# Second layer's key steps behind the links of its queries' chain, and two value chunks between its last first maxima

## The chip, the cores and the metric

The kernel runs on one core of one Trainium2 chip. The metric is the device time of one execution in microseconds; lower is better. The engines are TensorE (PE in the rows, its weight loads PEld), VectorE (DVE), ScalarE (ACT), GpSimd (POOL) and SyncE (SP), which issues the transfers.

## The reference

Two layers of a small perceiver work on 64 tokens x of 128 features and a context of 6272 rows. Each layer adds three blocks to x: cross-attention to the context, self-attention, and a mixture of experts.

```python
x = x + xattn0(layernorm(x), ctx)      # 16 heads of 8; q = y Wq + bq, k = ctx Wk + bk, v = ctx Wv + bv
x = x + attn0(layernorm(x))            # causal, 16 heads of 64
x = x + ffn0(layernorm(x))             # 8 experts, top 2, and a gated shared one
x = x + xattn1(layernorm(x), ctx)      # as xattn0, with q and k of each head normalised:
                                       #   qh = layernorm(qh, q_gamma, q_beta) * scale; kh = layernorm(kh, k_gamma, k_beta)
x = x + attn1(layernorm(x))            # rotary
x = x + ffn1(layernorm(x))             # 32 experts, top 1, and a shared one
```

The change lies where `ffn0` ends and `xattn1` begins.

## The kernel before

The context stands transposed in SBUF, 49 tiles of 128 rows, worked in NB = 13 chunks of up to 512 columns (the last has one tile). Each engine has its own instruction stream, written out by hand; the order in a stream is the order of the work, and semaphores tie the streams together.

**Keys of the second layer.** They don't depend on x, so they are made in steps that are placed among the serial links of `attn0` and `ffn0`. There are STEPS = 28. Step 2c is key chunk c: TensorE multiplies it (two records of 512 columns), ScalarE writes it twice, scaled into `klo` and squared into `khi`. Step 2c+1 is variance chunk c-1: TensorE averages the squares within each head, ScalarE turns them by Ln and Exp into 1/std (`k_rstd`). Then GpSimd multiplies (`k_scaled`, line 389), and VectorE adds beta, rounds and splits the result into a high and a low part (lines 581 and 584, `k_split`), after which SyncE copies both into the stacked form `kst`. On TensorE and ScalarE, `keys_until(n)` does the steps up to n that aren't done yet; the tables `PE_KEYS` and `ACT_KEYS` say up to which step at which named place. `DVE_KEYS` does so by chunks for VectorE. `PE_KEYS_IN_MAXIMA` and `DVE_KEYS_IN_MAXIMA` do it behind or ahead of the numbered pairs of the first maxima.

**Queries of the second layer.** After `ffn0`, x is normalised and transposed (`yT_of("ln3")`, copied by VectorE at line 539). TensorE multiplies by the centred query weights (`q1_ps`), ScalarE squares (line 493, `q1_sq`), TensorE averages (`q1_var`), ScalarE does Ln and Exp (lines 496, 497, `q1_std`), VectorE scales, adds beta and splits (lines 744 to 747, `q1_n`), TensorE spreads the result over rows (`query_rows`), and VectorE and ScalarE copy half each into `qst` (lines 544 and 449, `q_ready`).

**First maxima.** For head group 0, 13 pairs of score matmuls (`max_pair`) give each query's maximum over a chunk; VectorE reduces each pair (line 548). Between the pairs TensorE makes key steps and value chunks (`VALUES_IN_MAXIMA`), which ScalarE copies into `vaug` (`v_out`, line 402). `VALUE_BANKS` gives each value chunk's PSUM bank. Then come the shift (the maximum is subtracted from the queries) and the steps of the main loop (`cross`): scores, exponential (line 436), weighted sum, while the maxima of the next group run in slots of their own (line 554). The last LAST_V = 2 value chunks stand in the loop's first step, behind the first scores; scores 0 wait until all but these are copied, scores 1 until all are.

**Fill.** `keep_busy(n, free)` issues n matmuls of 256 columns into the free bank `free`; their result isn't used.

SyncE's order in the second layer: stack copies of groups 0 and 1, then the expert weights for the end of the kernel, then the stack copies of groups 2 and 3.

Of the kernel before, what the change touches and what calls it, by code (L numbers as in the profile page):

```python
# [16 lines left out]
NG = 4  # L17
# [104 lines left out]
def score_user(B):  # L122
# [5 lines left out]


STEPS = 2 * (NB + 1)  # L130
PE_KEYS = {"drain": 1, "o": 3, "x1": 6, "yT1": 7, "scores": 10, "probs": 11, "z": 12, "proj": 15, "ln2": 17, "y": 19,
           "yT3": 20, "q1": 21, "n1": 23}
PE_KEYS_IN_MAXIMA = {1: 24, 2: 25, 3: 26, 5: STEPS}
ACT_KEYS = {"drain": 3, "scores": 7, "vs": 12, "tab": 13, "sig": 17, "ln3": 19, "var": 20}
DVE_KEYS = {"ln1": 1, "qk": 2, "turned": 3, "z": 4, "h": 5, "hT": 6, "q1": 7, "n1": 8}
DVE_KEYS_IN_MAXIMA = {0: 9, 2: 10, 4: 11, 5: 12, 6: NB}

VALUE_BANKS = (5, 6, 3, 3, 1, 0, 1, 0, 1, 0, 1, 3, 2)
VALUES_IN_MAXIMA = {1: (2,), 3: (3,), 5: (4, 5), 6: (6,), 7: (7,), 8: (8,), 9: (9,), 12: (10,)}

ONE_VAR_BANK = 10
def var_bank(c):
# [6 lines left out]
def v_schedule(c):  # L149


    done = [0, 0, 1, 1, 2, 2] + [2 + min(6, -(-2 * n // 3)) + max(0, 3 * (n - 8) // 4) for n in range(NB)] + [NB - LAST_V]
    at = c + KEYS_AHEAD
    return range(done[at - 1] if at else 0, done[at] if c + 1 < NB else NB - LAST_V)

LAST_V = 2


def v_bank(l, c):
# [25 lines left out]
def perceiver(nc, ctxT, packs, experts, out):  # L187
    with ExitStack() as ctx:
# [202 lines left out]
        def _(act):  # L391
# [7 lines left out]
            def v_out(l, c):  # L399
                k = tiles(c)  # L400
                act.wait_ge(v_proj, l * NB + c + 1)
                nc.scalar.activation(vaug[:, BT * c:BT * c + k, :, 0:DH],  # L402
                                     ps[:, v_bank(l, c), 0:k * D].rearrange("p (t h d) -> p t h d", t=k, h=H),
                                     ACT.Copy).then_inc(v_set, 1)
# [22 lines left out]
            def exps(l):  # L427
                for g in range(NG):
                    for i in range(NB):
                        G = NG * l + g  # L430
                        B = G * NB + i
                        if B >= PROBS:
                            act.wait_ge(av_done, B - PROBS + 1)
                        act.wait_ge(scores_done, B + 1)
                        b0, w = score_bank(B), tiles(i) * P
                        nc.scalar.activation(prob[:, B % PROBS, :].rearrange("p (u c) -> p u c", u=2)[:, :, 0:w],  # L436
                                             ps[:, b0:b0 + 2, 0:w], ACT.Exp, scale=XSCALE).then_inc(exp_done, 1)
                        if g >= 1 and i == 0:
                            act.wait_ge(av_done, NB * G)
                            if G >= 2:  # L440
                                act.wait_ge(o_ready, G - 1)
                            nc.scalar.activation(avsb[:, :], ps[:, ACC, 0:GQ], ACT.Copy).then_inc(acc_copied, 1)
                        if g == 0 and i == 0:
                            for v in range(NB - LAST_V, NB):
                                v_out(l, v)
            def stack_queries(l):
                act.wait_ge(ev(f"q{l}_rows"), 1)
# [39 lines left out]
            nc.scalar.preload_act_table_set("natural_log_exp_and_others")  # L487
            keys_until(ACT_KEYS["sig"])
            v_out(1, 0)
            norm_std("ln3")  # L490
            keys_until(ACT_KEYS["ln3"])
            act.wait_ge(ev("q1_ps"), 1)
            nc.scalar.activation(q_n[:, 0:T], ps[:, 4, GQ:GQ + T], ACT.Square, bias=bq1c[:, 0:1]).then_inc(ev("q1_sq"), 1)
            keys_until(ACT_KEYS["var"])
            act.wait_ge(ev("q1_var"), 1)
            link(nc.scalar.activation(q_n[:, T:2 * T], ps[:, 4, GQ + T:GQ + 2 * T], ACT.Ln, bias=eps_col[:, 0:1]))
            nc.scalar.activation(q_n[:, T:2 * T], q_n[:, T:2 * T], ACT.Exp, scale=-0.5).then_inc(ev("q1_std"), 1)
            v_out(1, 1)
            stack_queries(1)
            keys_until(24)  # L500
            v_out(1, 2)
            keys_until(26)
            v_out(1, 3)
            keys_until(STEPS)
            for c in range(4, NB - LAST_V):
                v_out(1, c)
            exps(1)
            norm_std("ln4")
# [335 lines left out]
        def _(pe):  # L844
# [81 lines left out]
            def scores(G, i):  # L926
                B = NB * G + i
                if i == 0:
                    pe.wait_ge(shift_ready, 2 * (G + 1))
                if G % NG == 0 and i == 1:  # L930

                    pe.wait_ge(v_set, (G // NG + 1) * NB)
                if G % NG == 0 and i == 0:
                    pe.wait_ge(v_set, G // NG * NB + NB - LAST_V)
                elif G % NG == NG - 1 and i == 2:

                    pe.wait_ge(max_read, (G // NG + 1) * READS_OF_LAYER)
                elif score_user(B) is not None:
                    pe.wait_ge(exp_done, score_user(B) + 1)
                for t in range(tiles(i)):  # L940
                    a = (BT * i + t) * P
                    for p in range(2):
                        r = slice(p * HALF, (p + 1) * HALF)
                        last = one(ps[:, score_bank(B) + p, t * P:(t + 1) * P], kst[r, G % 2, a:a + P],
                                   qst[r, G % NG, p * P:(p + 1) * P])
                last.then_inc(scores_done, 1)
# [24 lines left out]
            def cross(l, wv):  # L971
                G0 = NG * l
                for s in range(EARLY_SLOTS):
                    max_slot(l, s)
                before = []
                for n, (front, back) in enumerate(STEP_SLOTS):
                    g, j = divmod(n, len(STEPS_OF_GROUP))
                    here = [(G0 + g, i) for i in STEPS_OF_GROUP[j]]
                    for s in front:
                        max_slot(l, s)  # L980
                    for G, i in here:
                        scores(G, i)
                    if n == 0:
                        for v in range(NB - LAST_V, NB):
                            v_chunk(l, v, wv)
                    for m, s in enumerate(back):
                        max_slot(l, s)
                        if n == 0:

                            if m == 0:  # L990
                                pe.wait_ge(v_set, (l + 1) * NB - 1)
                            keep_busy(2, 3)
                    for G, i in before:
                        weighted(G, i)
                    if j == 1 and g >= 1:
                        gather(G0 + g - 1)
                    if l == 1 and g == NG - 1 and j == 1:
                        pe.wait_ge(max_read, 2 * READS_OF_LAYER)
                        nc.tensor.transpose(ps[:, 7, 0:T], view["bv1"], ident[0:T, 0:T]).then_inc(ev("bias1_T"), 1)
                    if l == 1 and g == NG - 1 and j == 2:  # L1000
                        pe.wait_ge(ev("bias1_Ts"), 1)
                        one(ps[0:T, 7, D:2 * D], attT[:, :], view["wp1"]).then_inc(ev("bias1_out"), 1)
                    if l == 0 and g == NG - 1 and j == 1:

                        pe.wait_ge(in_pack["raw1"], 16)
                        pe.wait_ge(max_read, READS_OF_LAYER)
                        one(ps[:, 7, 0:D], view["wk1"], view["cen"])
                        one(ps[:, 7, D:D + 1], view["cen"], view["bk1"])
                        for q in range(NG):
                            one(ps[q * GC:(q + 1) * GC, 7, D + 1:D + 2], view["cen"][0:QROWS, 0:GC], view["bq1x3"][:, q:q + 1])  # L1010
                        one(ps[QROWS:P, 7, D + 2:D + 4], ident[0:QROWS, 0:GC], view["qgb"])
                        one(ps[:, 7, D + 4:2 * D + 4], view["wq1"], view["cen"]).then_inc(ev("l1_ps"), 1)
                    before = here
                if l == 0:

                    pe.wait_ge(ev("l1_weights"), 1)
                    keys_until(PE_KEYS["drain"])
                for G, i in before:
                    weighted(G, i)
                if l == 0:  # L1020
                    keep_busy(1, 7)
                gather(G0 + NG - 1)
# [99 lines left out]
            last.then_inc(ev("ffn0_hT"), 1)  # L1122
            pe.wait_ge(in_pack["small1"], 16)
            v_chunk(1, 0, view["wv1"])
            keep_busy(1, 4)
            pe.wait_ge(ev("ffn0_hTs"), 1)
            for e in range(E0 + 1):
                hh, k = e // SL, e % SL
# [3 lines left out]
            keys_until(PE_KEYS["y"])  # L1132
            v_chunk(1, 1, view["wv1"])
            yT_of("ln3")
            keys_until(PE_KEYS["yT3"])
            one(ps[:, 4, GQ:GQ + T], wq1c[:, :], yT[:, :]).then_inc(ev("q1_ps"), 1)
            keys_until(PE_KEYS["q1"])
            pe.wait_ge(ev("q1_sq"), 1)
            one(ps[:, 4, GQ + T:GQ + 2 * T], view["avg"], q_n[:, 0:T]).then_inc(ev("q1_var"), 1)
            keys_until(PE_KEYS["n1"])  # L1140

            pe.wait_ge(v_set, NB + 2)

            pe.wait_ge(k_rstd, 9)
            keep_busy(2, 2)
            query_rows(1)
            keep_busy(2, 2)
            pe.wait_ge(q_ready, 4)
            for c in range(NB):
                max_pair(1, c)  # L1150
# [187 lines left out]
```

## Time and profile before

| | |
|---|---|
| runs | 308.15 us median of 3 (306.65 to 308.65) |
| profiled execution | 308.23 us |
| span of its trace | 306.4 us |
| mean granted clock of TensorE | 0.989 |
| busy: TensorE, VectorE, ScalarE, GpSimd | 285.7, 211.8, 170.9, 29.5 us |

The span runs from the first to the last instruction in the trace, and starts and ends inside the time. A busy time is that of one engine; the engines overlap, so the shares say little on what sets the end. Almost every TensorE instruction is recorded at line 847, the helper `one`, so it is told apart by its tiles: `arena,consts` is a variance chunk, `arena,wk1c` a key chunk, `small,arena` a value chunk, `kst,qst` with 512 columns a maxima pair, `consts` alone a fill.

### The profile page before, as it was taken

To read this page: it belongs to the slowest core of one execution; us is meant where nothing else is said; L and a number is where in the kernel's file an instruction comes from. 1 tells how busy PE (TensorE), PEld (TensorE's weight loads), DVE (VectorE), ACT (ScalarE), POOL (GpSimd) and SP (SyncE) were. 2 spreads that over 40 slices of the span, in tenths; PEclk is the share of its full clock that TensorE was granted. 3 is DMA by queue.
4 is the path that set the end of the run, shared out by engine and by line. 5 is a ranking of instruction groups with operands and counts; after the bars stand their busy time and mean duration, and the time that the engine had idled before them with its cause. 6 is when DMAs were issued, how large, how long until landed. Compare 5 with 4: busy or idle time off the path is not lost.

```text
span 306.4 us, 8390 instructions
## 1 busy us (share of the span) xinstructions
PE 285.7 (93%) x3619; PEld 204.1 (67%) x3619; DVE 211.8 (69%) x443; ACT 170.9 (56%) x236; POOL 29.5 (10%) x23
## 2 busy tenths in 40 slices
PE   8999999999999998998899879999999998989986
PEld 4545667778787873554547656777877786556765
DVE  3679979899895104767879975989989411457762
ACT  3654337767666786579778322776767695031000
POOL 7710000000000002151325000000000000000000
PEclk9999999999999999999999977999999999999999
DMA  7877996756600370203065699994679600000000
GB/s 240 318 152 150 189 206 135 149 114 120 125 2 2 105 340 0 49 22 89 0 128 90 138 291 424 338 249 116 119 157 497 297 3 4 0 0 2 1 2 4
DMA packets 8116, 41.12 MB, mean 134 GB/s; under 512 B 2192, under 2 KB 2512, under 8 KB 7568
## 3 DMA queue, kind: packets, MB, share of 16 engines
q1 hardware_dynamic: 7936, 40.32, 47.9%
q8 instruction: 28, 0.46, 0.6%
q10 hardware_dynamic: 144, 0.27, 0.3%
q14 instruction: 8, 0.07, 0.1%
HBM read 21.29 MB, written 0.03 MB: 70 GB/s over the span
## 4 chain that ended last, share of the span: by engine, by line
PE 71%; DVE 18%; ACT 4%; DMA 3%; issue 2%; SPq 1%; DVEq 0%; ACTq 0%
PE ps L847 70%; DVE mx L548 4%; DVE mx L554 2%; DVE arena L584 2%; DMA arena<-in_ctxT 2%; ACT prob L436 1%; DVE arena L581 1%; DMA kst<-arena 1%; DVE arena L590 1%; DVE vaug L837 0%; ACT arena L408 0%; ACT arena L425 0%; ACT arena L424 0%; DVE qst L560 0%; SPq L319 0%
## 5 line engine op out<-in xcount | busy, mean ns | idle before, releaser
L436 ACT ACTIVATE prob<-ps 128x1024 f32<-128x1024 f32 (+1 forms) x104 | 99.5, 975 | 43.3 <-PE ps L847 43.1
L554 DVE TENSOR_REDUCE mx<-ps 128x1 f32<-128x512 f32 (+1 forms) x156 | 95.1, 655 | 14.5 <-PE ps L847 10.1
L847 PEld LDWEIGHTS ps<-qst,kst 64*128 64x128 f32 x784 | 53.1, 188 | 6.7 <-issue 1.8
L847 PE MATMUL ps<-prob,vaug 128*18 128x128 f32 x1568 | 57.0, 274 | 0.1
L847 PE MATMUL ps<-kst,qst 64*128 64x512 f32 (+1 forms) x208 | 50.5, 483 | 6.3 <-DVE mx L554 2.4
L847 PE MATMUL ps<-qst,kst 64*128 64x128 f32 x784 | 54.5, 273 | 0.7 <-ACT prob L436 0.3
L847 PEld LDWEIGHTS ps<-prob,vaug 128*18 128x18 f32 x1568 | 41.0, 97 | 9.9 <-issue 6.8
L847 PEld LDWEIGHTS ps<-kst,qst 64*128 64x128 f32 x208 | 19.9, 184 | 25.7 <-issue 13.2
L548 DVE TENSOR_REDUCE mx<-ps 128x2 f32<-128x1024 f32 (+1 forms) x26 | 29.2, 1156 | 0.7 <-PE ps L847 0.4
L402 ACT ACTIVATE vaug<-ps 128x512 f32<-128x512 f32 (+1 forms) x26 | 14.6, 571 | 19.6 <-PE ps L847 19.5
L847 PE MATMUL ps<-consts 128*128 128x256 f32 (+2 forms) x78 | 23.1, 416 | 0.0
L389 POOL TENSOR_TENSOR arena<-arena 128x512 f32<-128x512 f32 (+1 forms) x13 | 16.4, 1264 | 36.4 <-ACT arena L425 36.4
L847 PEld LDWEIGHTS ps<-consts 128*128 128x128 f32 (+1 forms) x78 | 13.5, 194 | 5.0 <-issue 2.1
L847 PE MATMUL ps<-arena,vaug 128*64 128x256 f32 (+1 forms) x184 | 15.6, 327 | 1.0 <-DVE vaug L837 0.8
L847 PEld LDWEIGHTS ps<-arena,vaug 128*64 128x64 f32 x184 | 12.8, 137 | 3.8 <-DVE vaug L837 1.3
L847 PEld LDWEIGHTS ps<-small,arena 128*128 128x128 f32 x98 | 13.0, 205 | 3.1 <-issue 1.4
L847 PE MATMUL ps<-small,arena 128*128 128x128 f32 x98 | 14.6, 298 | 0.1
L847 PE MATMUL ps<-arena,w 128*128 128x512 f32 (+1 forms) x26 | 13.9, 632 | 0.4 <-DVE arena L590 0.3
L847 PE MATMUL ps<-arena,consts 128*128 128x512 f32 (+1 forms) x26 | 13.6, 605 | 0.7 <-DVE yT L539 0.3
L575 DVE COPY avsb<-ps 128x256 f32<-128x256 f32 x2 | 0.8, 424 | 19.4 <-PE ps L847 19.4
L847 PEld LDWEIGHTS ps<-w,arena 128*128 128x128 f32 x98 | 12.0, 191 | 3.1 <-issue 2.9
L847 PE MATMUL ps<-w,arena 128*128 128x128 f32 x98 | 13.9, 285 | 0.0
(214 smaller groups left out, 267.7 us busy)
## 6 DMA issues: line engine op xcount, KB each, us to landing
kst<-arena SPq DMA_DIRECT2D x48, 192.0 KB, 3.6
kst<-arena SPq DMA_DIRECT2D x48, 128.0 KB, 2.7
arena<-in_experts SPq DMA_DIRECT2D x1, 5760.0 KB, 18.5
kst<-arena SPq DMA_DIRECT2D x24, 144.0 KB, 3.2
w<-in_experts SPq DMA_DIRECT2D x1, 3456.0 KB, 11.8
w<-in_late SPq DMA_DIRECT2D x1, 3284.5 KB, 11.4
arena<-in_experts SPq DMA_DIRECT2D x1, 3072.0 KB, 14.2
arena<-in_ctxT SPq DMA_DIRECT2D x2, 768.0 KB, 8.1
```

Source lines behind the costliest of these rows:

```text
L389: nc.gpsimd.tensor_tensor(klo[:, a:b], klo[:, a:b], khi[:, a:b], ALU.mult).then_inc(k_scaled, 1)
L402: nc.scalar.activation(vaug[:, BT * c:BT * c + k, :, 0:DH], ps[:, v_bank(l, c), 0:k * D].rearrange("p (t h d) -> p t h d", t=k, h=H), ACT. ...
L436: nc.scalar.activation(prob[:, B % PROBS, :].rearrange("p (u c) -> p u c", u=2)[:, :, 0:w], ps[:, b0:b0 + 2, 0:w], ACT.Exp, scale=XSCALE). ...
L548: V.tensor_reduce(mx[:, :, k], ps[:, pair_bank(k):pair_bank(k) + 2, 0:width(k)], AX, ALU.max).then_inc(max_read, 1)
L554: V.reduce_max(mx[:, p, k:k + 1], ps[:, bank(s, p), 0:width(k)], AX).then_inc(max_read, 1)
L575: V.tensor_copy(avsb[:, :], ps[:, ACC, 0:GQ]).then_inc(acc_copied, 1)
L581: V.tensor_scalar(khi[:, a:b].bitcast(F32R), klo[:, a:b], view["kgb"][:, 1:2], None, ALU.add).then_inc(k_full, 1)
L584: V.scalar_tensor_tensor(klo[:, a:b], klo[:, a:b], view["kgb"][:, 1:2], khi[:, a:b], ALU.add, ALU.subtract).then_inc(k_split, 1)
L590: V.scalar_tensor_tensor(klo[:, a:b], ps[:, c % 2, 0:width(c)], view["bk0"], khi[:, a:b], ALU.add, ALU.subtract).then_inc(k_split, 1)
L847: return mm(out_, lhsT, rhs, start=start, stop=stop, skip_group_check=True)
```

## The change

Four edits, all in the second layer.

- Steps on TensorE: variance chunk 7 (step 17) takes the place of the fill behind value chunk 0; key chunk 9 and variance chunk 8 (steps 18, 19) stand behind the last matmuls of `ffn0`; no step stands between the transposed input and the query matmul, or between this and the average; steps 20 and 21 come behind the average, step 22 behind the query rows. The wait for `k_rstd` 9 and the four fills around the query rows go.
- Steps on ScalarE: step 17 comes ahead of the norm's Ln, step 18 stays behind it, and step 19 goes from ahead of the queries' Ln to behind value chunk 1's copy.
- Value chunk 10 goes from behind pair 12 to behind pair 11, and chunk 11 from the first step of the loop to behind pair 12. `LAST_V` becomes (2, 1), one number for each layer.
- In the first step of the second layer's loop, the fill is 3 matmuls behind each of two slots instead of 2.

```diff
-PE_KEYS = {"drain": 1, "o": 3, "x1": 6, "yT1": 7, "scores": 10, "probs": 11, "z": 12, "proj": 15, "ln2": 17, "y": 19,
-           "yT3": 20, "q1": 21, "n1": 23}
+PE_KEYS = {"drain": 1, "o": 3, "x1": 6, "yT1": 7, "scores": 10, "probs": 11, "z": 12, "proj": 15, "ln2": 17, "hT": 18,
+           "y": 20, "n1": 22, "rows": 23}
 PE_KEYS_IN_MAXIMA = {1: 24, 2: 25, 3: 26, 5: STEPS}
-ACT_KEYS = {"drain": 3, "scores": 7, "vs": 12, "tab": 13, "sig": 17, "ln3": 19, "var": 20}
+ACT_KEYS = {"drain": 3, "scores": 7, "vs": 12, "tab": 13, "sig": 17, "v0": 18, "ln3": 19, "v1": 20}
-VALUES_IN_MAXIMA = {1: (2,), 3: (3,), 5: (4, 5), 6: (6,), 7: (7,), 8: (8,), 9: (9,), 12: (10,)}
+VALUES_IN_MAXIMA = {1: (2,), 3: (3,), 5: (4, 5), 6: (6,), 7: (7,), 8: (8,), 9: (9,), 11: (10,), 12: (11,)}
...
-LAST_V = 2
+LAST_V = (2, 1)
...
             keys_until(ACT_KEYS["sig"])
             v_out(1, 0)
+            keys_until(ACT_KEYS["v0"])
             norm_std("ln3")
             keys_until(ACT_KEYS["ln3"])
             act.wait_ge(ev("q1_ps"), 1)
             nc.scalar.activation(q_n[:, 0:T], ps[:, 4, GQ:GQ + T], ACT.Square, bias=bq1c[:, 0:1]).then_inc(ev("q1_sq"), 1)
-            keys_until(ACT_KEYS["var"])
             act.wait_ge(ev("q1_var"), 1)
...
             v_out(1, 1)
+            keys_until(ACT_KEYS["v1"])
             stack_queries(1)
...
-                    pe.wait_ge(v_set, G // NG * NB + NB - LAST_V)
+                    pe.wait_ge(v_set, G // NG * NB + NB - LAST_V[G // NG])
...
-                        for v in range(NB - LAST_V, NB):
+                        for v in range(NB - LAST_V[l], NB):
                             v_chunk(l, v, wv)
...
-                            keep_busy(2, 3)
+                            keep_busy(2 + l, 3)
...
             v_chunk(1, 0, view["wv1"])
-            keep_busy(1, 4)
+            keys_until(PE_KEYS["hT"])
             pe.wait_ge(ev("ffn0_hTs"), 1)
...
             yT_of("ln3")
-            keys_until(PE_KEYS["yT3"])
             one(ps[:, 4, GQ:GQ + T], wq1c[:, :], yT[:, :]).then_inc(ev("q1_ps"), 1)
-            keys_until(PE_KEYS["q1"])
             pe.wait_ge(ev("q1_sq"), 1)
             one(ps[:, 4, GQ + T:GQ + 2 * T], view["avg"], q_n[:, 0:T]).then_inc(ev("q1_var"), 1)
             keys_until(PE_KEYS["n1"])
 
             pe.wait_ge(v_set, NB + 2)
-
-            pe.wait_ge(k_rstd, 9)
-            keep_busy(2, 2)
             query_rows(1)
-            keep_busy(2, 2)
+            keys_until(PE_KEYS["rows"])
             pe.wait_ge(q_ready, 4)
```

The other uses of `LAST_V` follow in the same way.

## Rows read from the trace of the kernel before

**Rows 1.** The page: clock in 40 slices, then the chain by engine and line.

```profile
PEclk9999999999999999999999977999999999999999
...
PE 71%; DVE 18%; ACT 4%; DMA 3%; issue 2%; SPq 1%; DVEq 0%; ACTq 0%
PE ps L847 70%; DVE mx L548 4%; DVE mx L554 2%; DVE arena L584 2%; DMA arena<-in_ctxT 2%; ACT prob L436 1%; DVE arena L581 1%; DMA kst<-arena 1%; DVE arena L590 1%; DVE vaug L837 0%; ACT arena L408 0%; ACT arena L425 0%; ACT arena L424 0%; DVE qst L560 0%; SPq L319 0%
```

**Rows 2.** Timeline, 146 to 159 us: start, us, engine, line, instruction.

```profile
146.11 0.60 PE L847 MATMUL ps<-consts 128*128 128x256 f32 x2
...
147.45 1.31 PE L847 MATMUL ps<-w,prob 128*64 128x128 f32 x18 [0.74 <-DVE prob L736]
...
150.43 0.29 ACT L453 ACTIVATE lnv<-mv,eps_col 64x1 f32<-64x1 f32 x1 [1.77 <-DVE mv L534]
...
151.80 0.22 DVE L539 COPY yT<-ps 128x64 f32<-128x64 f32 x1 [0.40 <-PE ps L863]
...
152.08 1.12 PE L847 MATMUL ps<-arena,consts 128*128 128x512 f32 x2 [0.32 <-DVE yT L539]
...
153.41 0.31 ACT L493 ACTIVATE prob<-ps,bq1c 128x64 f32<-128x64 f32 x1
...
154.87 0.30 ACT L496 ACTIVATE prob<-ps,eps_col 128x64 f32<-128x64 f32 x1
...
155.81 0.55 DVE L745 TENSOR_SCALAR qhl<-prob,qgb 128x64 fp32r<-128x64 f32 x1
...
156.28 0.30 DVE L746 TENSOR_SCALAR prob<-prob,qgb 128x64 f32<-128x64 f32 x1
...
156.62 0.23 DVE L747 TENSOR_TENSOR qhl<-prob,qhl 128x64 fp32r<-128x64 f32 x1
...
157.06 0.53 PE L847 MATMUL ps<-qhl,spread 32*128 32x64 f32 x12
...
157.94 0.84 DVE L544 CAST qst<-ps 32x256 fp32r<-32x256 f32 x2
```

**Rows 3.** Busy us by stage, columns PE, PEld, DVE, ACT, POOL, clock, DMA, GB/s.

```profile
158.80:180.00 21.20, 17.83 (x106) 12.21 (x106) 20.64 (x26) 12.26 (x23) 4.41 (x4) 1.00 0.69 132
```

**Rows 4.** Busy us of six stretches, columns as in rows 3.

```profile
181.30:189.01 7.71, 7.71 (x30) 5.47 (x30) 3.53 (x6) 1.79 (x3) 0.00 (x0) 0.59 0.93 394
39.40:44.40 5.00, 4.96 (x30) 3.44 (x30) 3.53 (x6) 1.79 (x3) 0.00 (x0) 1.00 1.00 234
189.01:242.60 53.59, 51.84 (x947) 41.19 (x947) 47.06 (x88) 37.12 (x40) 0.00 (x0) 1.00 0.85 272
44.40:97.96 53.56, 51.81 (x947) 41.19 (x947) 47.05 (x88) 37.11 (x40) 0.00 (x0) 1.00 0.46 96
177.00:181.30 4.30, 2.54 (x19) 1.49 (x18) 3.59 (x8) 0.60 (x1) 0.00 (x0) 0.93 1.15 274
...
292.50:296.70 4.20, 3.08 (x24) 1.69 (x20) 3.28 (x10) 0.47 (x1) 0.00 (x0) 1.00 0.00 0
```

**Rows 5.** One microsecond on TensorE: busy us, granted clock, DMA share, GB/s.

```profile
181.00:182.00 1.00, 0.88 (x9) 0.50 1.27 429
```

**Rows 6.** The chain of waits: a two-record matmul with nothing ahead.

```profile
273.46 0.45 PE ps L847 x2
```

**Rows 7.** Timeline, 132 to 135 us: VectorE and GpSimd meet.

```profile
132.85 0.75 DVE L584 SCALAR_TENSOR_TENSOR arena<-arena,consts 128x512 f32<-128x512 f32 x1
...
133.15 1.60 POOL L389 TENSOR_TENSOR arena<-arena 128x512 f32<-128x512 f32 x1 [1.21 <-ACT arena L425]
```

**Rows 8.** Timeline, the end of the first maxima.

```profile
176.83 2.69 DVE L548 TENSOR_REDUCE mx<-ps 128x2 f32<-128x1024 f32 x3 [0.24 <-PE ps L847]
178.11 0.33 PE L847 MATMUL ps<-kst,qst 64*128 64x128 f32 x2 [0.97 <-DVE mx L548]
178.37 1.16 PE L847 MATMUL ps<-small,arena 128*128 128x128 f32 x8
...
180.19 0.41 PE L847 MATMUL ps<-consts,mhl 128*32 128x128 f32 x4 [0.66 <-DVE mhl L569]
```

More of the change, by code:

```diff
@@ L149, in v_schedule @@
 def v_schedule(c):
-    done = [0, 0, 1, 1, 2, 2] + [2 + min(6, -(-2 * n // 3)) + max(0, 3 * (n - 8) // 4) for n in range(NB)] + [NB - LAST_V]
+    done = [0, 0, 1, 1, 2, 2] + [2 + min(6, -(-2 * n // 3)) + max(0, 3 * (n - 8) // 4) for n in range(NB)] + [NB - LAST_V[0]]
     at = c + KEYS_AHEAD
-    return range(done[at - 1] if at else 0, done[at] if c + 1 < NB else NB - LAST_V)
-LAST_V = 2
+    return range(done[at - 1] if at else 0, done[at] if c + 1 < NB else NB - LAST_V[0])
+LAST_V = (2, 1)
 def v_bank(l, c):
@@ L504, in _ @@
             keys_until(STEPS)
-            for c in range(4, NB - LAST_V):
+            for c in range(4, NB - LAST_V[1]):
                 v_out(1, c)
@@ L983, in cross @@
                     if n == 0:
-                        for v in range(NB - LAST_V, NB):
+                        for v in range(NB - LAST_V[l], NB):
                             v_chunk(l, v, wv)
```

## The prediction

> **What bounds the kernel now.** I read the page's chain first: the tensor engine holds 71% of the chain that ended last and VectorE 18% [rows 1]. So a gain must come from a stretch where VectorE or a serial chain sets the pace, or where TensorE is slow. The clock row of the same page shows one such place: the granted clock is below full in two slices, about 176 to 191 us, and nowhere else inside the work [rows 1]. Then I read the timeline between the first layer's last stage and the second layer's first scores, because the whole change lies there. It has three parts.
>
> The **queries' chain** (149 to 159 us) is serial: normalised x is turned, multiplied by the query weights, squared, averaged, put through Ln and Exp, scaled, spread over rows and copied into qst. Key steps stand in front of its links. The turned input is ready at 152.02 (151.80 + 0.22), but TensorE first runs a variance chunk (152.08, 1.12 us), so the square of the queries starts only at 153.41; another key chunk stands before the average matmul, and the Ln starts at 154.87 [rows 2]. In the **first maxima** (158.8 to 180) VectorE is busy 20.64 of 21.20 us [rows 3]: it sets the pace, and whatever moves its first instruction moves the end. Then the **first scores**: from 181.30 to 189.01 TensorE takes 7.71 us for 30 matmul records. The first layer does the same work, same count, in 5.00 us (39.40 to 44.40) at full clock; here the mean granted clock is 0.59 [rows 4]. From 181 to 182 us the level is 0.50 (1.2 instead of 2.4 GHz) [rows 5], so the fall comes just before the first scores. Before it TensorE was busy for only 2.54 of 4.30 us (177.00 to 181.30) [rows 4]: it waits for the last first maxima and then for the shift.
>
> Behind 189.01 the layers are alike: 53.59 us against 53.56 to the end of their maxima [rows 4]. So what is won ahead of 189.01 should stay won.
>
> **The profiled execution** took 308.23 us for a span of 306.4, so 1.8 lie around the span; it is within 0.1 us of the median, 308.15. I sum against 308.23. A difference below about 1% (3.1 us) is what a measurement of this kernel hardly tells from none.
>
> **Part 1: the fill matmul behind the first value chunk becomes a variance chunk.** The fill costs some 0.53 us, the chunk some 1.1. It stands in a wait: value chunk 0 is through at about 146.2, the fill behind it (its first records at 146.11) ends at 146.71, and the matmuls that wait for hTs start at 147.45 [rows 2], so 1.1 us just fit. Price 0, up to 0.1 if the fit fails. Its Ln and Exp on ScalarE now come before the norm's Ln: ScalarE idles 1.77 us before that Ln [rows 2], they take 1.3. GpSimd's product for that key chunk then falls at about 150.0 to 151.3, beside VectorE's norm. The y instruction starts at 151.06 and would be held by at most the 0.25 us that L745 lost beside GpSimd (0.55 against 0.30 for the same shape) [rows 2]; I take 0, since the other work is short and reads ahead of GpSimd's end. The Trainium skill (GPSIMD Engine Reference, section 1, Specifications) says that GpSimd shares its SBUF interface with VectorE and contends with two-port modes and with instructions with two SBUF inputs. By that rule y may wait and the sum would be up to 0.25 worse.
>
> **Part 2: the queries' links no longer wait for key steps.** A two-record matmul with nothing in front took 0.45 us [rows 6]. So the square starts at 152.02 + 0.05 + 0.45 = 152.5 (before 153.41), and the Ln at 152.8 + 0.05 + 0.45 = 153.3 (before 154.87): 1.55 us. ScalarE must be free: its key chunk 9 starts right behind the norm at 150.9 and takes 1.35, done by 152.2. L745 ran beside GpSimd; GpSimd's next product is now later, so 0.25 comes on top: L747 ends at 156.85 - 1.55 - 0.25 = 155.05 [rows 2]. On TensorE key chunk 10 and variance chunk 9 now stand between the average matmul and the query rows: 153.25 + 2 x 0.93 = 155.1, just ready. With them go the wait for k_rstd and four fills. The query rows start 1.95 earlier than 157.06 [rows 2]. On VectorE key chunk 7 stands before its qst copies as before, so the copies end 1.8 earlier than 158.78 (157.94 + 0.84) [rows 2].
>
> What is late next: the product for key chunk 8. Its Ln and Exp now follow the queries' and value chunk 1 on ScalarE: 153.9 + 0.55 + 1.3 = 155.7. GpSimd starts then, beside VectorE's L584 of chunk 7 (155.5 to 156.25). In the like place GpSimd ended at 134.75 (133.15 + 1.60), 1.15 us behind an L584 that ended at 133.60 [rows 7]: so 157.4. VectorE, free at 157.0, starts chunk 8 at 157.45, against 158.81 (0.03 behind its copies). **Gain 1.4 us.** Key steps 20 to 23 on ScalarE follow the stack copies as before and come about 1.9 us earlier, so they don't hold VectorE later. One collision is left: the products of chunks 9 to 12 come earlier relative to VectorE by 0.5 us, and a meeting of the two stretches one of them, as here GpSimd's to 1.60 [rows 7]; there are such meetings now as well, so I take 0 and keep a loss of up to 0.9 for the range. Bounds of this part: 0 (all of it eaten by the two engines meeting) and 1.95 (the whole advance of the query rows).
>
> **Part 3: value chunk 10 a place earlier, chunk 11 behind the last first maxima.** Chunk 10 (8 records, 1.16 us) [rows 8] now goes between pairs 11 and 12. Pair 12 starts at 178.11 and would then start at about 178.2, while VectorE's last three reductions run from 176.83 to 179.52 without a gap, the last of them, pair 12's, a short one of some 0.35 [rows 8]: hidden, with 0.6 to spare. Chunk 11 runs from 178.55 to 179.7; the shift's matmul waits for VectorE until 180.19 anyway [rows 8]. The scores at 181.30 now wait for chunk 11's copy as well: 179.7 + 0.6 = 180.3, done. Without that cover each costs up to 1.1 us. In the first scores 8 records of a chunk go and two fills come (3 instead of 2, twice): 1.06 us out, 1.06 in, at full clock. Cost 0. The second scores wait for the copy of chunk 12, ready before, as it is now one short copy behind the first exponential.
>
> **Part 4: the clock.** With the two chunks TensorE's waits between 177.1 and 181.3 shrink from 1.76 us (4.30 - 2.54) to about 0.9: busy share 0.59 before, about 0.8 after. The trace shows full clock through 4.20 us with 3.08 busy (0.73, from 292.50) [rows 4]. So I take it that the clock stays up, and the first scores take the first layer's 5.00 us: **gain 2.7 us**. Bounds: 0 (still falls) and 2.7. Inside the new queries' chain the fills are gone, and two waits of 0.4 us and one of 0.3 lie within 151.7 to 153.3; key chunks fill both sides, so the busy share there stays above 0.7.
>
> The rule that speaks against the change is in TensorE: Matmul & The Clock Gate, Part 1: the Trainium skill says that the gated clock is the default, that only activity releases it, and that the monitor runs free of the kernel's start. By it the taking away of fills can cost the clock elsewhere, and the same program can fall in one execution and not in the next. The sum would then be 306.8 instead of 304.1.
>
> **Transfers.** SyncE's stack copies of the second layer wait for k_split, which comes with VectorE's key chunks: 1.4 earlier, like the pairs that read them. The expert loads follow them in SyncE's order, one of them behind the last value copy, and the stacks of groups 2 and 3 follow those. TensorE's need for these moves 4.1 us earlier and their issue follows the scores that free their slots, but the loads ahead of them move by only 1.4 to 4. If they landed just in time now, up to 2.7 us would be at risk; but the second layer, with the expert loads in the queue, is only 0.03 us longer behind 189.01 than the first, which has none there [rows 4], and DMA holds 3% of the chain, of which the stacks 1% [rows 1]. I take 0.
>
> **Sum.** 308.23 - 1.4 - 2.7 = 304.1 us.
>
> **Rivals.**
> - *The clock gain alone, 305.5.* The queries' chain moves but VectorE doesn't, as GpSimd's products or ScalarE's Ln and Exp come late. For: my margins at chunk 8 and at the query rows are under 0.5 us. Against: VectorE has at most these two waits.
> - *The queries' gain alone, 306.8.* The clock falls as before or at a neighbouring wait. For: a wait of 0.5 us before the shift and 0.3 behind it remain. Against: a busy share of 0.73 was enough elsewhere [rows 4].
> - *It doesn't do what it says, 308.2.* VectorE's reductions start where they did and the clock falls.
> - *Slower, 309.5.* The lost fills: with four fills and the chunks in front of the links gone, the clock falls in the queries' chain at about 153 as well. Price as in the one fall in the trace: 2.7 us each (7.71 against 5.00). If the fall at 181 also stays: 308.2 - 1.4 + 2.7 = 309.5; it decides against the change once two falls stand where one was. Two falls added would give 312.2.
>
> **How the numbers follow.** Forecast 0.60, clock alone 0.12, queries alone 0.17, nothing 0.05, slower 0.06. The forecast's own width is 303.0 to 305.1 (queries' part 0.5 to 1.95, chunks' cover 0 to 0.5). The range reaches to both partial cases: 302.9 to 307.1, leaving out the last two and the tails. Faster by over 1% (under 305.1): nearly all of the forecast and a little of the clock case, 0.58. Slower by over 1% (over 311.3): half of the slow case, 0.03. Within: 0.39.
>
> **What would show it.** Right: the square about 0.5 us behind the turned copy, the Ln about 0.8 behind the square; first reduction of the maxima near 158.7; full clock from 176 to 190; about 5.0 us from the first scores to the second; the second half unchanged in length. Wrong: a half-clock stretch anywhere between 150 and 190, GpSimd named before VectorE's L581 of chunk 8 by more than 0.5 us, a VectorE wait before pair 12 or the shift, or ScalarE's value copy named before the first scores.

## The result and the profile after

| | median | lowest to highest | executions |
|---|---|---|---|
| before | 308.70 us | 306.65 to 312.20 | 20 |
| after | 307.69 us | 305.15 to 315.02 | 20 |

The ratio is 0.9936, 95% interval 0.9911 to 0.9961; like the ratios below it leaves out executions far above the fastest of their kernel (over 1.5%), of which the changed one has more (5 of 20 against 1), so it is better than the ratio of the medians, 0.9967. The change gains about 0.6%, some 2 us, where I forecast 4.1. The profiled execution of the changed kernel took 310.19 us (span 308.4). It is longer than the median. Up to the second scores it agrees within 0.1 us with a second trace of the same kernel (e1 below), and it shows plainly what comes then.

The page, as in [rows 1]: the clock in 40 slices, then the chain of waits by engine and line.

```profile
PEclk9999999999999999999999999958999999999999
...
PE 69%; DVE 16%; DMA 7%; ACT 3%; issue 2%; SPq 1%; POOL 1%; DVEq 0%; ACTq 0%
PE ps L848 68%; DMA kst<-arena 5%; DVE mx L549 3%; DVE mx L555 2%; DMA arena<-in_ctxT 2%; DVE arena L585 2%; ACT prob L436 1%; DVE arena L582 1%; SPq L319 1%; DVE arena L591 1%; POOL arena L389 1%; DVE vaug L838 0%; ACT arena L408 0%; DVE yT L540 0%; PE ps L864 0%
```

The half-clock slices are no longer at 176 to 191 but three slices later, about 200 to 216, and DMA has risen from 3% to 7% of the chain, 5% of it `kst<-arena`, the stack copies. Up to the second scores everything lies where it was forecast. The timeline of the queries' chain, answering [rows 2]:

```profile
149.87 1.26 POOL L389 TENSOR_TENSOR arena<-arena 128x512 f32<-128x512 f32 x1 [1.69 <-ACT arena L425]
...
151.71 0.23 DVE L540 COPY yT<-ps 128x64 f32<-128x64 f32 x1 [0.40 <-PE ps L864]
...
152.46 0.32 ACT L494 ACTIVATE prob<-ps,bq1c 128x64 f32<-128x64 f32 x1 [0.36 <-PE ps L848]
...
153.30 0.31 ACT L496 ACTIVATE prob<-ps,eps_col 128x64 f32<-128x64 f32 x1 [0.53 <-PE ps L848]
...
154.26 0.31 DVE L746 TENSOR_SCALAR qhl<-prob,qgb 128x64 fp32r<-128x64 f32 x1
...
155.20 0.53 PE L848 MATMUL ps<-qhl,spread 32*128 32x64 f32 x12 [0.16 <-DVE qhl L748]
...
155.71 1.65 POOL L389 TENSOR_TENSOR arena<-arena 128x512 f32<-128x512 f32 x1 [4.57 <-ACT arena L425]
...
156.15 0.83 DVE L545 CAST qst<-ps 32x256 fp32r<-32x256 f32 x2
...
157.39 0.49 DVE L582 TENSOR_SCALAR arena<-arena,consts 128x512 fp32r<-128x512 f32 x1 [0.40 <-POOL arena L389]
...
158.69 2.36 DVE L549 TENSOR_REDUCE mx<-ps 128x2 f32<-128x1024 f32 x2
```

The square starts at 152.46 (forecast 152.5), the Ln at 153.30 (153.3), L746, which was L745, takes 0.31 instead of 0.55, and VectorE waits 0.40 for GpSimd's product (forecast 0.45) before chunk 8. The first reduction of the maxima starts at 158.69 instead of 160.12: 1.43 us, forecast 1.4. VectorE still sets the pace of that stage; its row, in the columns of [rows 3]:

```profile
157.00:180.00 23.00, 19.79 (x122) 13.54 (x122) 21.42 (x28) 12.94 (x24) 5.24 (x5) 1.00 0.75 153
```

The end of the first maxima in the timeline, answering [rows 8]:

```profile
175.74 1.16 PE L848 MATMUL ps<-small,arena 128*128 128x128 f32 x8
176.82 0.19 PEld L848 LDWEIGHTS ps<-kst,qst 64*128 64x128 f32 x2
176.82 0.33 PE L848 MATMUL ps<-kst,qst 64*128 64x128 f32 x2
...
177.08 1.16 PE L848 MATMUL ps<-small,arena 128*128 128x128 f32 x8
...
178.86 0.41 PE L848 MATMUL ps<-consts,mhl 128*32 128x128 f32 x4 [0.62 <-DVE mhl L570]
```

Chunk 10 fits ahead of pair 12, chunk 11 behind it, and the shift's matmul waits for VectorE as before. The stretches that answer to [rows 4], in its columns:

```profile
175.70:179.97 4.27, 3.38 (x27) 2.46 (x26) 3.56 (x8) 1.20 (x2) 0.00 (x0) 1.00 1.08 249
179.97:184.95 4.98, 4.98 (x28) 3.40 (x28) 3.87 (x6) 1.19 (x2) 0.00 (x0) 1.00 0.91 378
184.95:200.99 16.04, 13.15 (x244) 10.37 (x245) 12.51 (x23) 10.14 (x10) 0.00 (x0) 0.97 0.99 366
200.99:210.90 9.91, 9.77 (x100) 7.28 (x100) 5.31 (x10) 3.11 (x5) 0.00 (x0) 0.54 0.43 108
```

TensorE is busy for 3.38 of 4.27 us ahead of the first scores (before 2.54 of 4.30), the clock stays at 1.00, and the first scores take 4.98 us, not 7.71. The second scores, with their slot, start at 184.95, 4.1 us earlier than at 189.01. Then the gain goes. The stretch to 200.99 holds an idle time, which single microseconds show (TensorE's busy us, granted clock, DMA share, GB/s):

```profile
198.00:199.00 1.00, 0.36 (x16) 1.00 1.05 412
199.00:200.00 1.00, 0.00 (x0) 0.95 1.07 338
200.00:201.00 1.00, 0.01 (x2) 0.50 0.92 244
201.00:202.00 1.00, 1.00 (x8) 0.50 1.01 199
```

TensorE stands still for 2.6 us, then works at half clock. The chain of waits at that place (start, us, what):

```profile
185.82 0.48 SPq L319
186.34 0.61 SPq L319
186.99 13.95 DMA kst<-arena
200.99 4.78 PE ps L848 x45
```

SyncE issues the three copies of the first stack piece of group 2, the last of them takes 13.95 us to land, and the first maxima slot of group 2 starts at 200.99, where it could have started near 198.3, behind the weighted sum that ends at 198.36 (e2, below, starts it at 198.20).

### The profile page after: what moved, and what is told of

The parts are those of the page before. It is cut to its first block, busy times and chain, and to the rows that moved or that the text cites. A ratio compares the mean times of both kernels' runs of the same rounds, so it can differ in the third digit from the quotient of the medians.

```text
span 308.4 us, 8378 instructions
## 1 busy us (share of the span) xinstructions
PE 285.2 (92%) x3613; PEld 203.7 (66%) x3613; DVE 210.9 (68%) x443; ACT 171.1 (55%) x236; POOL 30.3 (10%) x23
## 4 chain that ended last, share of the span: by engine, by line
PE 69%; DVE 16%; DMA 7%; ACT 3%; issue 2%; SPq 1%; POOL 1%; DVEq 0%; ACTq 0%
PE ps L848 68%; DMA kst<-arena 5%; DVE mx L549 3%; DVE mx L555 2%; DMA arena<-in_ctxT 2%; DVE arena L585 2%; ACT prob L436 1%; DVE arena L582 1%; SPq L319 1%; DVE arena L591 1%; POOL arena L389 1%; DVE vaug L838 0%; ACT arena L408 0%; DVE yT L540 0%; PE ps L864 0%
## 5 line engine op out<-in xcount | busy, mean ns | idle before, releaser
L848 PE MATMUL ps<-prob,vaug 128*18 128x128 f32 x1568 | 58.9, 279 | 0.1
L848 PE MATMUL ps<-kst,qst 64*128 64x512 f32 (+1 forms) x208 | 51.3, 490 | 8.2 <-DMA kst<-arena 3.2
L848 PEld LDWEIGHTS ps<-qst,kst 64*128 64x128 f32 x784 | 54.0, 191 | 6.8 <-issue 1.8
L848 PEld LDWEIGHTS ps<-prob,vaug 128*18 128x18 f32 x1568 | 41.9, 99 | 10.6 <-issue 7.0
L402 ACT ACTIVATE vaug<-ps 128x512 f32<-128x512 f32 (+1 forms) x26 | 14.7, 571 | 18.3 <-PE ps L848 18.2
L389 POOL TENSOR_TENSOR arena<-arena 128x512 f32<-128x512 f32 (+1 forms) x13 | 17.2, 1327 | 34.3 <-ACT arena L425 34.3
L848 PE MATMUL ps<-consts 128*128 128x256 f32 (+2 forms) x72 | 20.3, 402 | 0.0
L848 PEld LDWEIGHTS ps<-consts 128*128 128x128 f32 (+1 forms) x72 | 12.1, 187 | 4.0 <-issue 2.3
L848 PEld LDWEIGHTS ps<-small,arena 128*128 128x128 f32 x98 | 12.0, 191 | 3.3 <-issue 1.7
L848 PE MATMUL ps<-small,arena 128*128 128x128 f32 x98 | 13.7, 283 | 0.1
L848 PE MATMUL ps<-arena,wk1c 128*128 128x512 f32 (+1 forms) x26 | 13.5, 601 | 0.3 <-DVE yT L540 0.3
## 6 DMA issues: line engine op xcount, KB each, us to landing
arena<-in_experts SPq DMA_DIRECT2D x1, 3072.0 KB, 18.2
```

The source lines that it names most:

```text
L389: nc.gpsimd.tensor_tensor(klo[:, a:b], klo[:, a:b], khi[:, a:b], ALU.mult).then_inc(k_scaled, 1)
L402: nc.scalar.activation(vaug[:, BT * c:BT * c + k, :, 0:DH], ps[:, v_bank(l, c), 0:k * D].rearrange("p (t h d) -> p t h d", t=k, h=H), ACT. ...
L848: return mm(out_, lhsT, rhs, start=start, stop=stop, skip_group_check=True)
```

## The wait that I priced at nothing

In the kernel before, the same slot is this row of the timeline:

```profile
202.47 0.50 PE L847 MATMUL ps<-kst,qst 64*128 64x512 f32 x2
```

And these are the three copies of its piece (durations are of the issue; below them the times from issue to landing):

```profile
L319 SPq DMA_DIRECT2D kst<-arena x3: 475/594/597, 190.0 to 191.1; - x3
...
DMA to landing us min/median/max: 8.9/9.0/9.3
```

They are issued from 190.0 to 191.1 and land 8.9 to 9.3 us later, the last at 200.4 at the latest. The slot starts at 202.47, so the slack was 2 us; TensorE's need moved forward by 4.1, and the landing (200.9 after) not at all. The reason is what lies ahead of the piece in SyncE's order, as e8 will show. The two expert loads, before (start and length of the issue, then KB and us from issue to landing):

```profile
178.87 0.82 SPq L323 DMA_DIRECT2D w<-in_experts  x1
185.24 0.33 SPq L323 DMA_DIRECT2D arena<-in_experts  x1
...
w<-in_experts SPq DMA_DIRECT2D x1, 3456.0 KB, 11.8
arena<-in_experts SPq DMA_DIRECT2D x1, 3072.0 KB, 14.2
```

and after:

```profile
177.68 0.77 SPq L323 DMA_DIRECT2D w<-in_experts  x1
181.95 0.33 SPq L323 DMA_DIRECT2D arena<-in_experts  x1
...
w<-in_experts SPq DMA_DIRECT2D x1, 3456.0 KB, 12.6
arena<-in_experts SPq DMA_DIRECT2D x1, 3072.0 KB, 18.2
```

The first lands at about 190.7 before and 190.3 after (issue plus the last column). The second lands at 199.4 before and 200.15 after: an issue 3.3 us earlier only stretched it from 14.2 to 18.2. From 182 to 200 us the DMA engines are busy throughout in both kernels (share 0.99 and 1.00, at 391 and 385 GB/s), and the piece lands behind the load.

## The experiments

In the tables below, the span at full clock is the median of the spans of executions with a mean granted clock of 0.999 or more (their number of all). Half-clock time is 2 x (1 - mean clock) x span, averaged over all executions of that kernel. Ratios are to the kernel before on the same chip. The three sets ran on three chips, and the kernel before differed between them (medians 308.4, 310.2 and 308.0), so medians are compared within a set; where the text sets half-clock times or full-clock spans of two sets side by side, the difference may be partly one of the chips.

**The first set: the order of the transfers.**

`e1_after` is the changed kernel.

> The changed kernel itself, once more, beside the others on one chip. Transfer theory: the steps up to the second scores of the second layer gain 4.1 us (second scores near 185 instead of 189), and then TensorE waits for the first stack piece of group 2, which lies behind the expert weights in SyncE's order: some 1 to 3 us near 198. In an undisturbed execution the gain left is about 3 us, in many less, because the clock falls behind that wait. Lost-fill theory: the losses are clock falls between 150 and 182 us, in the queries' chain, and the wait near 198 plays no part.

`e2_after_experts_last` moves the first two expert loads behind all stack copies:

```diff
             for k in range(len(KC) + 1):
                 ...
-            sp.wait_ge(ev("ffn0_y"), 1)
-            load_experts(1, NEAR, E1)
-            sp.wait_ge(v_set, 2 * NB)
             first = S // EW
-            load_experts(0, 0, first)
...
             load("tail1")
+            load_experts(1, NEAR, E1)
+            load_experts(0, 0, first)
             load_experts(2, first, NEAR)
```

> The changed kernel with the first two expert loads moved behind all stack copies, so that no stack piece lies behind them. Transfer theory: the wait near 198 is gone, with it the clock fall behind it, and the whole 4.1 us stay: ratio to before near 0.987, median near 304.5, with less spread. Lost-fill theory: ratio as in the changed kernel, 0.993, with the same falls of the clock. A third way: the expert loads now end too late for the experts near 278 us, and the kernel is slower.

`e3_before_experts_last` is the same edit on the kernel before.

> The kernel before with the same move of the expert loads. Transfer theory: nothing waits for a stack piece in the kernel before, so the ratio is 1.000, within 0.2%; the half-clock stretch at 181 stays. If the move is worth something by itself (less contention, or fewer clock falls), the ratio here shows how much of the run before must be put down to it.

`e4_keys_only` is the changed kernel with the value chunks, `LAST_V` and the fills of the first scores as before:

```diff
-VALUES_IN_MAXIMA = {..., 9: (9,), 11: (10,), 12: (11,)}
+VALUES_IN_MAXIMA = {..., 9: (9,), 12: (10,)}
-LAST_V = (2, 1)
+LAST_V = (2, 2)
-                            keep_busy(2 + l, 3)
+                            keep_busy(2, 3)
```

> Only the key steps of the change (parts 1 and 2); value chunks and fills of the first scores as before. By my sum 1.4 us earlier at the first reduction of the maxima, and the clock still falls at 181: about 306.8 in an execution like the profiled one, ratio 0.995 to 0.997. The need for the stack of group 2 comes 1.4 earlier, which the old slack still covers: no wait near 200. Lost-fill theory: the time is no better than before, with more half-clock time.

| | ratio, 95% | median us | span at full clock | half-clock time |
|---|---|---|---|---|
| before | | 308.39 | 305.2 (6 of 35) | 6.7 |
| e1, after | 0.9936 (0.9886 to 0.9985) | 308.59 | none of 12 (303.3 and 303.5 in the first 20) | 8.4 |
| e2, after, experts last | 0.9894 (0.9856 to 0.9932) | 305.46 | 302.7 (6 of 12) | 2.6 |
| e3, before, experts last | 0.9947 (0.9908 to 0.9985) | 306.36 | 304.1 (4 of 12) | 3.2 |
| e4, keys only | 0.9959 (0.9920 to 0.9998) | 307.28 | 304.2 (2 of 12) | 6.0 |

The slot of group 2 in e1 (timeline, TensorE; in brackets the idle time before and its releaser):

```profile
197.20 1.07 PE L848 MATMUL ps<-prob,vaug 128*18 128x128 f32 x32
199.66 0.50 PE L848 MATMUL ps<-kst,qst 64*128 64x512 f32 x2 [1.39 <-DMA kst<-arena]
```

and in e2, where no expert load lies ahead of the piece:

```profile
197.20 1.07 PE L846 MATMUL ps<-prob,vaug 128*18 128x128 f32 x32
198.20 0.50 PE L846 MATMUL ps<-kst,qst 64*128 64x512 f32 x2
```

The wait is gone, and the span of this execution is 302.4, my 306.4 - 4.1 to 0.1 us. Its page has no half-clock slice:

```profile
PEclk9999999999999999999999999999999999999999
```

The transfer theory holds: the wait goes with the loads ahead of it. The order is worth 1.3 us by the ratios (0.9936 to 0.9894, with intervals that overlap) and 3.1 in the medians (308.59 to 305.46), where e1's longest executions count too. The expert loads, now last, aren't waited for in the traces of e2 and e11. The theory didn't foresee e3. The kernel before also gains from it, 1.1 us at full clock and 2.0 in the median, where I expected none. e3's profiled execution has no half-clock slice either, not even at 181, where the kernel before had two:

```profile
PEclk9999999999999999999999999999999999999999
```

Its span is 304.0, 2.4 under the 306.4 of before, with the fall's cost gone and no other change in the tensor work. So the fall at 181 that I priced is not in every execution. In the kernel before, executions with the mean clock of the profiled one (0.989, 16 of 35) have a span of 306.5, and those without any fall one of 305.2. Only 1.3 us lie between them, not 2.7. With the loads last (e3) the same two groups are at 306.5 and 304.1, 2.4 apart. That the lower clock is in each of them the fall at 181 is my inference, as only the profiled ones can be looked into. So what is missing from the 2.7 at full clock is a wait for the piece, 1.1 us: the expectations of e9 follow from that.

e4 missed its expectation of no wait near 200. Its trace has one:

```profile
PE ps L848 <- DMA kst<-arena: 1.5, 1, 1.5
```

The clock stayed at 1.00 at 181 in this execution, without the value chunks in their new places, so TensorE came to the piece as early as in the changed kernel, waited, and the clock fell behind the wait (0.57 from 200 to 204 us).

**The second set: parts with the transfers out of the way, and the wait itself.**

`e5_keys_only_experts_last` is e4 with the transfers of e2.

> The key steps of the change alone, with both first expert loads behind all stack copies. Here no transfer can take the gain back. In executions at full clock the span is 1.4 to 1.5 us under that of the kernel before with the same transfers (304.0), so 302.6; the value chunks add nothing to it. If the value chunks have a gain of their own besides the clock, it is missing here and the span stays above that of the whole change (302.4) by more than 0.3.

`e6_values_only_experts_last` is the kernel before with the value chunks, `LAST_V` = (2, 1), the third fills, and the transfers of e2.

> The value chunks and the third fills alone, with both expert loads last. Theory that chunks only guard the clock: at full clock the span is 304.0, as in the kernel before with the same transfers, and fewer executions have a half-clock stretch than its mean of 3.2 us. Rival: they do nothing for the clock either, mean half-clock time 3 us or more.

`e7_after_fill_in_wait` puts work into the wait:

```diff
                 if kind == "max":
-                    stack_there(G, k)
+                    if (l, g, k) != (1, 2, 0):
+                        stack_there(G, k)
                     pe.wait_ge(max_read, reads_before(l, 0) + max(0, uses(SLOTS[:s]) - 1))
+                    if (l, g, k) == (1, 2, 0):
+                        keep_busy(4, bank(s))
+                        stack_there(G, k)
```

> The changed kernel with four fill matmuls (2.1 us) in the place where TensorE waits for the first stack piece of group 2; the transfers as in the changed kernel. If the clock falls because TensorE idles in that wait: mean half-clock time drops from 8.4 us to near that with the expert loads last (2.6), and the median falls by 1.5 to 3 us although the wait itself stays. If the falls come from elsewhere (the lost fills of the queries' chain): half-clock time as before, and the time rises by the part of the fills that the wait doesn't cover, 0 to 1 us.

`e8_after_one_piece_first` moves the second expert load (with its wait for the value copies) behind the first stack piece of group 2:

```diff
             load_experts(1, NEAR, E1)
-            sp.wait_ge(v_set, 2 * NB)
             first = S // EW
-            load_experts(0, 0, first)
             for g in (2, 3):
                 for k in range(len(KC)):
                     stack(1, g, k)
+                    if (g, k) == (2, 0):
+                        sp.wait_ge(v_set, 2 * NB)
+                        load_experts(0, 0, first)
```

> The changed kernel with the second expert load (3.07 MB) behind the first stack piece of group 2 instead of ahead of it; the first expert load stays where it was. Transfer theory: the first piece lands some 9 us earlier and its wait near 198 is gone, but the pieces behind the load can be late in its place, 8 to 10 us behind their issue: time between the changed kernel and that with both loads last. If instead the mere issue of transfers or their volume at that time were the cost, not their order, it would be as in the changed kernel.

| | ratio, 95% | median us | span at full clock | half-clock time |
|---|---|---|---|---|
| before | | 310.22 | none of 22 | 9.2 |
| e5, keys only, experts last | 0.9901 (0.9859 to 0.9942) | 306.37 | 302.4 (3 of 12) | 5.5 |
| e6, values only, experts last | 0.9904 (0.9867 to 0.9940) | 306.08 | 303.9 (5 of 8) | 1.5 |
| e7, fill in the wait | 0.9916 (0.9883 to 0.9949) | 306.90 | 305.1 (7 of 10) | 2.2 |
| e8, one piece first | 0.9857 (0.9809 to 0.9905) | 305.22 | 302.4 (1 of 6) | 4.2 |

With the transfers out of the way the spans at full clock add up: 304.1 with neither part, 302.4 with the key steps, 303.9 with the value chunks, 302.7 with both. The key steps are worth 1.2 to 1.7 us and the value chunks about nothing in time. Whether these guard the clock isn't shown. Half-clock time is 5.5 without them and 2.6 with them (e5, e2), 3.2 and 1.5 on the old key steps (e3, e6). e5's profiled execution has the fall in the old place:

```profile
PEclk9999999999999999999999978999999999999999
```

The same four numbers would say that moving the key steps costs clock (3.2 to 5.5, 1.5 to 2.6). All these differences rest on 8 to 12 executions each, partly on different chips, and I don't rely on them. The traces speak against a reliable guard. Of the nine with the value chunks in their new places, three (e7, e9, e11) have a fall within the first scores; of the four without, two (before, e5). This is e11, whose TensorE was as busy ahead of the first scores as that of the changed kernel (3.39 of 4.27 us from 176.07, against 3.38 of 4.27); its clock is 0.50 from 182 to 185 us:

```profile
PEclk9999999999999999999999998999999999999999
```

And e3 and e4 kept the full clock there with 2.42 and 2.39 of 4.30 us busy, less than the 2.54 behind which it fell in the kernel before.

e7 tells the wait from what follows it. TensorE there, four fills and then the slot with no idle time:

```profile
199.91 2.01 PE L848 MATMUL ps<-consts 128*128 128x256 f32 x8
201.85 0.50 PE L848 MATMUL ps<-kst,qst 64*128 64x512 f32 x2
```

The slot starts later than in the changed kernel (200.99 and 199.66), some 1.6 us of it because this execution had a fall from about 181.6 to 185.0, and at full clock the span is 1.7 us longer than the 303.4 of the changed kernel (the fills' 2.0 exceed the wait). Yet half-clock time is 2.2 us, where the kernel before has 9.2 in this set and e1 8.4 in the first, and 7 of 10 executions ran at full clock, against 2 of 32 of the changed kernel (its first 20 and e1's 12). The clock stays at 1.00 behind the slot (201.85 to 211). In the three traces in which TensorE idled for 1.39 us or more there (the changed kernel, e1 and e4), it fell within the wait or right behind it. So idling in this wait is what brings the clock down behind it. Whether the fills gain time isn't shown: the ratios, 0.9916 and 0.9936, have intervals that overlap. The lost-fill theory of the queries' chain falls with this: the fills lost there are missing in e7 too, and none of the 13 traces has a fall between 149 and 159 us.

e8 gets the gain with one piece moved, with the same volume of transfers: it is the order that counts. TensorE still waits once, for the second piece (us in total, times, longest):

```profile
PE ps L849 <- DMA kst<-arena: 0.6, 1, 0.6
```

**The third set: the value chunks in the old order, and the two better versions side by side.**

`e9_values_only` is e6 with the transfers as before.

> The value chunks and third fills alone, with the transfers in their old order. They keep the clock up at 181, so TensorE comes to the first stack piece of group 2 some 2.7 us earlier than in the profiled execution of before. Transfer theory: it then waits there by some 1 us (need near 199.5 against a landing near 200 to 201), the full-clock span is that of the kernel before at full clock, 305.1, and not the 303.9 with the expert loads last; falls of the clock behind that wait take the place of those at 181. Rival (a wait arises only from the key steps' advance): no wait, 304.

`e10_after_one_piece_first` is e8 again, `e11_after_experts_last` is e2 again.

> The changed kernel with only the first stack piece of group 2 ahead of the second expert load, again, now on one chip with the version with both loads last. Full-clock span 302.4 to 303.4 (a late second piece costs 0.6 in some executions), half-clock time 2.5 to 4 us, ratio 0.986 to 0.990.

> The changed kernel with both expert loads last, again, for the comparison with the version with one piece first: full-clock span 302.4, half-clock time near 2.6 us, ratio 0.987 to 0.990; no worse than the other, since no piece at all waits behind a load here.

| | ratio, 95% | median us | span at full clock | half-clock time |
|---|---|---|---|---|
| before | | 308.02 | 304.9 and 305.3 (2 of 17) | 6.7 |
| e9, values only | 1.0005 (0.9972 to 1.0039) | 310.48 | 304.5 (1 of 12) | 7.9 |
| e10, one piece first | 0.9891 (0.9855 to 0.9927) | 304.91 | 302.8 (5 of 6) | 3.7 |
| e11, experts last | 0.9898 (0.9866 to 0.9931) | 305.21 | 302.9 (3 of 6) | 1.8 |

e9 is the plainest of all. The part on which I put 2.7 us gives 1.0005 by itself. It didn't keep the clock up at 181 in the profiled execution, against my expectation. Its trace has the wait for the piece, 0.49 us in this execution, whose clock had fallen before (mean 0.76 from 182 to 189), so that TensorE came to the slot near 201.8 and not near 199.5, as I had expected at full clock (the one execution at full clock, 304.5, lies between the 305.1 and the 304 of the two theories and decides nothing):

```profile
200.72 1.07 PE L847 MATMUL ps<-prob,vaug 128*18 128x128 f32 x32
202.28 0.50 PE L847 MATMUL ps<-kst,qst 64*128 64x512 f32 x2 [0.49 <-DMA kst<-arena]
```

With the expert loads last (e6) it was 0.9904, against 0.9947 for the loads alone (e3), a difference within the intervals. e10 and e11 can't be told apart; both beat the kernel before, by 1.1% and 1.0%. That they beat the changed kernel (0.9936) is likely and not shown by the ratios, whose intervals overlap a little.

## Why the prediction was wrong

- **Part 1** held: the variance chunk fits the fill's place, and y isn't held beside GpSimd (0.34 us before and after). GpSimd's product ends 0.16 us behind y's start, so the two hardly met, and the rule of the Trainium skill (GPSIMD Engine Reference, section 1, Specifications) on contention was hardly tried on y.
- **Part 2** held in each link: 1.43 us at the first reduction, forecast 1.4; with the transfers out of the way the key steps bring 1.2 to 1.7 (e6 to e2, e3 to e5).
- **Part 3** held: both chunks are hidden, the first scores take 4.98 us.
- **Part 4** came true in the profiled execution (clock 1.00, 4.98 us) and failed as a term of the sum. I took the 2.7 us between two layers of one execution for the gain of every execution. The kernel before has executions without that fall; at full clock it takes 305.2 against 304.1 with the loads last, so it seems to come to the group-2 piece early and to wait there (no trace shows such an execution). That capped the gain of avoiding the fall at about 1.3 us (306.5 to 305.2). Nor is it shown that the chunks keep the clock up: it fell in e7 and e11 with the same busy share ahead of it. That the profiled execution kept it was in part luck.
- **Transfers** is the step that failed first, where I wrote "I take 0". I argued that a stage of equal length in both layers (53.59 and 53.56 us) shows that no piece was late, and it wasn't; but it says nothing about the slack, which was 2 us against a need that moved by 4.1. I had named up to 2.7 us at risk and then left it out of the sum and of the rivals. It measured 2.6 us in the profiled execution, 1.4 in e1, and some 0.7 at full clock (303.4 against 302.7). By the ratios of e1 and e2 it cost 1.3 of the 2.1 us that the change fell short; the rest I put down to the term of part 4.
- **What I had not priced**: the wait itself idles TensorE, and the clock falls behind it. The fall at 181 that I meant to save came back at 200. Half-clock time was 6.7 us before, and 6.8 in the first 20 executions of the changed kernel and 8.4 in e1's 12: no less. What is left is about the gain at full clock, 1.8 us (305.2 to 303.4), near the 2 us of the ratio.
- **The rivals.** The rule of the Trainium skill (TensorE: Matmul & The Clock Gate, Part 1), that only activity releases the clock and that the monitor runs free of the kernel's start, fits: the same program ran with no half-clock time and with over 20 us of it. But none of my four named the transfer, and the nearest, a clock that falls at a neighbouring wait, had the wrong wait. The slower rival, falls in the queries' chain, isn't in any of the traces, and e7 speaks against it.

The forecast's 304.1 is near what the changed kernel reaches with the transfers out of its way and the clock up: 302.7 + 1.8 = 304.5 for e2, whose medians, with the clock falls that remain, are 305.5 and 305.2 (e11).

## What to carry to other kernels

When a change moves an engine earlier, list the next things that it will need, and for each the slack between landing and need, from the trace; a wait that isn't there now says only that the slack is above zero. A transfer that a full queue holds doesn't come earlier for being issued earlier: the large loads ahead of it must go, and here one load moved behind one small piece was worth about as much as the change itself (0.9936 became 0.9857 in e8 and 0.9891 in e10). And a loss that one profiled execution shows at the clock isn't a term of the median before several executions show it; the mean granted clock of each is the quickest way to see that.

## What the runs showed that I had not expected

- A single wait of 1.4 to 2.6 us on TensorE costs twice: its length, and then half-clock time (0.97 and 0.54 mean clock in the two stretches above). With four fill matmuls in it, 2.0 us long, the mean half-clock time was 2.2 us instead of 8.4, although at full clock they make the kernel 1.7 us longer.
- The same program with the same work ahead of the first scores kept the full clock there in some traces (the changed kernel, e1) and lost it in another (e7).
- The expert loads' order is worth 0.5% to the kernel before too (0.9947), with nothing else changed.
- A load issued 3.3 us earlier landed 0.7 us later (200.15 against 199.44).
